# Second weight matrix loaded and used in two halves, all down projections ahead of all up projections, and the last batch's residual finished inside the recurrence

## The reference

```
c = layernorm(cond) * gamma + beta
w = gelu(c @ W1 + bias1) @ W2 + bias2            # W2 is 256 x 8192, 8 MB
a1, b1, a2, b2 = split(w, 4)                     # each [B, D, 8], per batch
mid = gelu(x @ base_down + (x @ a2) @ b2.T)      # "down"
out = mid @ base_up.T + (mid @ b1) @ a1.T        # "up"
x2  = x + (x + out)
for t in range(512):                             # recurrence over time, all 4 batches
    h = tanh(x2[:, t] @ Wx + b + h @ Wh)
    result[:, t] = x2[:, t] + h
```

## Time and profile before

| | |
|---|---|
| median of 3 runs | 568.85 us (566.21 to 568.97) |
| the profiled execution, its own time | 569.51 us |
| its span, first to last instruction | 567.6 us |
| PE busy | 510.9 us (90%) |
| DVE, ACT, POOL busy | 287.8, 173.9, 21.6 us |
| recurrence's first own product (L653) starts | 79.80 us |

### The profile page before, as it was taken

How to read it: one execution, slowest core, us unless ns; L and a number is a source line. 1 busy time by engine, 2 the same in 40 slices (tenths; PEclk the granted TensorE clock), 3 DMA queues, 4 the chain that set the end, 5 groups by cost and what they waited for, 6 DMA issues and landing times.

```text
span 567.6 us, 31977 instructions
## 1 busy us (share of the span) xinstructions
PE 510.9 (90%) x14200; PEld 429.1 (76%) x14200; DVE 287.8 (51%) x2214; ACT 173.9 (31%) x1128; POOL 21.6 (4%) x33
## 2 busy tenths in 40 slices
PE   4979989999999999999999999999999999999995
PEld 4334458888888888888888888888888888888884
DVE  2142355555555555555555555555555555555553
ACT  3021113333333333333333333333333333333322
POOL 1039100000000000000000000000000000000000
PEclk9978989999999999999999999999999999999999
DMA  7950000000000000000000000000000000000000
GB/s 259 387 190 0 0 3 4 4 13 5 13 4 13 4 14 4 13 5 10 8 3 14 3 14 3 14 3 14 3 14 3 13 5 14 3 11 6 6 13 12
DMA packets 11216, 15.99 MB, mean 28 GB/s; under 512 B 1587, under 2 KB 6978, under 8 KB 11074
## 3 DMA queue, kind: packets, MB, share of 16 engines
q1 hardware_dynamic: 11078, 13.95, 7.4%
HBM read 11.85 MB, written 2.10 MB: 25 GB/s over the span
## 4 chain that ended last, share of the span: by engine, by line
PE 82%; ACT 8%; issue 3%; SPq 3%; DMA 3%; DVE 0%; DVEq 0%
PE bank L653 66%; ACT w_sb L358 8%; PE bank L633 7%; PE bank L589 3%; DMA w_sb<-in_L_cond_W 3%; PE bank L601 2%; SPq L227 2%; PE bank L642 1%; PE bank L628 1%; PE bank L571 1%; PE bank L578 1%; PE bank L515 0%; PE bank L554 0%; ACT xT L315 0%; DVE x2T L446 0%
## 5 line engine op out<-in xcount | busy, mean ns | idle before, releaser
L653 PE MATMUL bank<-w_sb,whp 128*128 128x52 bf16 x6132 | 244.2, 186 | 38.7 <-ACT w_sb L358 38.0
L653 PEld LDWEIGHTS bank<-w_sb,whp 128*128 128x128 bf16 x6132 | 188.5, 96 | 86.8 <-ACT w_sb L358 64.5
L479 DVE TENSOR_TENSOR r_ring<-w_sb 128x4 f32<-128x4 f32 x1022 | 136.6, 164 | 220.9 <-ACT w_sb L358 218.5
L358 ACT ACTIVATE w_sb<-bank 128x4 f32<-128x4 f32 x1024 | 142.2, 174 | 324.7 <-PE bank L653 324.7
L653 PE MATMUL bank<-r_ring,whp 128*128 128x52 bf16 x4096 | 220.7, 186 | 0.0
L653 PEld LDWEIGHTS bank<-r_ring,whp 128*128 128x128 bf16 x4096 | 174.7, 96 | 0.0
L653 PE MATMUL bank<-l_ring,whp 128*128 128x52 bf16 (+1 forms) x2048 | 157.5, 178 | 0.0
L484 DVE TENSOR_TENSOR l_ring<-r_ring 128x4 bf16<-128x4 f32 x1024 | 135.9, 162 | 0.0
L653 PEld LDWEIGHTS bank<-l_ring,whp 128*128 128x128 bf16 x2048 | 122.3, 96 | 0.0
L633 PE MATMUL bank<-xp,wxp 128*128 128x32 bf16 x1536 | 76.2, 176 | 0.0
L633 PEld LDWEIGHTS bank<-xp,wxp 128*128 128x128 bf16 x1536 | 56.2, 95 | 0.0
(11 more groups left out here) (84 smaller groups left out, 147.6 us busy)
## 6 DMA issues: line engine op xcount, KB each, us to landing
w_sb<-in_L_cond_W SPq DMA_DIRECT2D x8, 1024.0 KB, 14.0
x_sb<-in_x SPq DMA_DIRECT2D x4, 512.0 KB, 9.6
out<-o_sb SPq DMA_DIRECT2D x64, 32.0 KB, 1.6
w_sb<-in_L_cond_W SPq DMA_DIRECT2D x1, 256.0 KB
up_sb<-in_L_cond_base_up SPq DMA_DIRECT2D x1, 256.0 KB, 3.1
down_sb<-in_L_cond_base_down SPq DMA_DIRECT2D x1, 256.0 KB, 11.1
wh_sb<-in_L_cond_Wh SPq DMA_DIRECT2D x1, 256.0 KB
wx_sb<-in_L_cond_Wx SPq DMA_DIRECT2D x1, 256.0 KB
```

The costliest lines, as they stand in the source:

```text
L358: nc.scalar.activation(h_ring[:, m, slot(pair, s), 0:B], zt, ACT.Tanh).then_inc(h_ready, 1)
L479: nc.vector.tensor_tensor(r_ring[:, k, q, 0:B], state_before(pair, s, k)[:, 0:B], state_hi_before(pair, s, k)[:, 0:B], ALU.subtract).then_ ...
L653: return nc.tensor.matmul(zbank(p, q, m)[:, col0:col0 + n], whp[part][:, k, P * m:P * (m + 1)], rhs[:, 0:n], start=False, stop=stop, skip_ ...
```

## The change

1. **W2 in two halves.** Types A2 and B2 of all chunks are loaded first (eight transfers of 0.5 MB), then x1, base_down, x2, x3, then A1 and B1 of all chunks. The PE's products follow: `w_products(0, c)` takes A2 and B2, `w_products(1, c)` A1 and B1. DVE's keep_rank works on the 64 partitions of one half.
2. **Two queues.** ACT issues cond, gamma, beta, bias2, W1, bias1, b, x0 and base_up at its start. SP starts with W2 at once. `ld_cond` is now cond alone; gamma and beta, and W1 and bias1, have semaphores of their own.
3. **Order on the PE.** The bias2 products go ahead of the first layer's. The x0 and base_up transposes stand between the first half's W products. All low_down, all down, the second half's W products between the downs, all low_up, then the four ups. midT lies over x_sb and has room for four batches; x transposes use two banks in place of three.
4. **The last batch's x2.** DVE makes only its first 64 steps (`FIRST`) ahead of the recurrence, and the other 448 in eight pieces of 112 in the steps 3 to 10 of the first pair.
5. **Smaller moves.** POOL makes quadrant and splits b first; the padding of h_ring comes last. ACT, not DVE, copies upT. DVE makes facm for A2 alone and b1m itself, a batch at a time, in place of one operation over all and ACT's copy.

```diff
+        HALVES = ((A2, B2), (A1, B1))
...
+            def load_w2(h):
+                j = min(HALVES[h])
+                for c in range(NCH):
+                    for k in range(K2):
+                        sp.dma_start(w2_sb[:, k, j:j + 2, CH * c:CH * (c + 1)],
+                                     w2v[k, :, j:j + 2, CH * c:CH * (c + 1)]).then_inc(ld_w2[h][c][k], 16)
+
+            load_w2(0)
+            load_x(1)
+            sp.dma_start(down_sb[:], base_down.rearrange("(k p) n -> p k n", p=P)).then_inc(ld_down, 16)
+            load_x(2)
+            load_x(3)
+            load_w2(1)
...
+            def w_products(h, c):
                 for k in range(K2):
-                    pe.wait_ge(ld_w2[c][k], 16)
-                    for j in range(NTYPE):
+                    pe.wait_ge(ld_w2[h][c][k], 16)
+                    for j in HALVES[h]:
                         last = nc.tensor.matmul(bank[c][Q * j:Q * (j + 1), :],
...
-            dve.wait_ge(ld_cond, 80)
+            dve.wait_ge(ld_cond, 16)
...
+                    if b < B - 1:
+                        make_x2(b, n, 0, T).then_inc(x2_ready, 1)
+                    else:
+                        make_x2(b, n, 0, FIRST).then_inc(x2_first, 1)
...
+                    if first and PIECE0 <= s < PIECE0 + PIECES * K2:
+                        n, i = (s - PIECE0) % K2, (s - PIECE0) // K2
+                        make_x2(B - 1, n, FIRST + (T - FIRST) // PIECES * i,
+                                FIRST + (T - FIRST) // PIECES * (i + 1)).then_inc(x2_rest, 1)
```

More of the change, by code:

```diff
@@ L130, in adaptive_lowrank_then_recurrence @@
         ld_cond = sem("ld_cond")
+        ld_gb = sem("ld_gb")
+        ld_w1 = sem("ld_w1")
         ld_bias2 = sem("ld_bias2")
         ld_x = [sem(f"ld_x{b}") for b in range(B)]
-        ld_base = sem("ld_base")
-        ld_w2 = [[sem(f"ld_w2_{c}_{k}") for k in range(K2)] for c in range(NCH)]
+        ld_down = sem("ld_down")
+        ld_up = sem("ld_up")
+        ld_w2 = [[[sem(f"ld_w2_{h}_{c}_{k}") for k in range(K2)] for c in range(NCH)] for h in range(2)]
+        ld_b = sem("ld_b")
         ld_rnn = sem("ld_rnn")
@@ L152, in adaptive_lowrank_then_recurrence @@
         upT_ready = sem("upT_ready")
-        ld_up = sem("ld_up")
-        w_ready = sem("w_ready")
-        facm_ready = sem("facm_ready")
+        w_ready = [sem(f"w_ready{h}") for h in range(2)]
+        a2_ready = sem("a2_ready")
         b1_ready = sem("b1_ready")
@@ L320, in _ @@
                                      bias=bias1_sb[:, m:m + 1]).then_inc(g_ready, 1)
-            for g in range(B * K2):
+            move_transposes(0)
+            move_transposes(1)
+            act.wait_ge(upT_psum, 1)
+            nc.scalar.copy(upT[:].rearrange("p k n -> p (k n)"), bank[6][:]).then_inc(upT_ready, 1)
+            for g in range(K2, B * K2):
                 move_transposes(g)
-            act.wait_ge(facm_ready, 1)
-            nc.scalar.copy(b1m[:], facm[Q * B1:Q * (B1 + 1)]).then_inc(b1_ready, 1)
             for b in range(B):
@@ L328, in _ @@
                     act.wait_ge(mid_psum, K2 * b + m + 1)
[L329 to L332, removed]
+                    nc.scalar.activation(midT[:, b, m, :], mid_bank(b, m)[:], ACT.Gelu).then_inc(mid_ready, 1)
             def x_part1(col0):
@@ L361, in states @@
                         if s % TS == 0:
+                            if 2 * pair + s // TS + 1 == FIRST // TS:
+                                act.wait_ge(x2_rest, PIECES * K2)
                             if 2 * pair + s // TS > 2:
@@ L424, in _ @@
-            dve.wait_ge(ld_base, 16)
-            def add_down(b):
+            for b in range(B):
+                nc.vector.tensor_scalar(facm[Q * A2:Q * (A2 + 1), b], fac[Q * A2:Q * (A2 + 1)],
+                                        bmask[Q * A2:Q * (A2 + 1), b:b + 1], None, ALU.mult).then_inc(a2_ready, 1)
+            dve.wait_ge(ld_down, 16)
+            for b in range(B):
                 dve.wait_ge(wd_psum, b + 1)
-                nc.vector.tensor_tensor(wd[:, b].rearrange("p k n -> p (k n)"), bank[4 + b][:],
+                nc.vector.tensor_tensor(wd[:, b].rearrange("p k n -> p (k n)"), low_bank(b)[:],
@@ L428, in add_down @@
                                         down_sb[:].rearrange("p k n -> p (k n)"), ALU.add).then_inc(wd_ready, 1)
-            def add_up(b):
+            for c in range(NCH):
+                keep_rank(1, c)
+            for b in range(B):
+                nc.vector.tensor_scalar(b1m[:, b], fac[Q * B1:Q * (B1 + 1)], bmask[Q * B1:Q * (B1 + 1), b:b + 1],
+                                        None, ALU.mult).then_inc(b1_ready, 1)
+            dve.wait_ge(upT_ready, 1)
+            for b in range(B):
@@ L508, in _ @@
             last.then_inc(condT_ready, 1)
-            def transposes(g):
-                if g >= 3:
-                    pe.wait_ge(tr_moved, g - 2)
-                for i in range(NTT):
-                    last = nc.tensor.transpose(tr_bank(g)[:, P * i:P * (i + 1)],
-                                               x_sb[:, g // K2, i, P * (g % K2):P * (g % K2 + 1)], ident[:])
-                last.then_inc(tr_ready, 1)
+            pe.wait_ge(ld_bias2, 16)
+            pe.wait_ge(quadrant_ready, 1)
+            for c in range(NCH):
+                nc.tensor.matmul(bank[c][:], quadrant[:].rearrange("j i q -> j (i q)"),
+                                 bias2_sb[:, CH * c:CH * (c + 1)], start=True, stop=False, skip_group_check=True)
             pe.wait_ge(cn_ready, 1)
@@ L688, in recurrence @@
                                 pe.wait_ge(o_ready, pair)
+                        if first and p == 0 and i == 4:
+                            pe.wait_ge(x2_rest, PIECES * K2)
                         input_products(1 - p, i // 4, i // 2 % 2, [i % 2])
```

210 lines of the change are left out of this document (110 added, 100 removed).

## The result

The changed kernel takes 572.86 us (median of 12 executions, 570.20 to 574.77), the kernel before 568.84 (12 executions, 566.21 to 569.52). The ratio is 1.0073, with a 95% interval of 1.0051 to 1.0096: slower by 4.0 us where 4.3 us less were forecast. The profiled execution of the changed kernel took 574.48 us, its span is 572.6.

The account below looks back on a forecast made before the run. The recurrence's start was taken as bound by W2's landing, the PE work behind it and TensorE's clock. Summed steps put the last x2 at 73.75 instead of 78.02, 4.3 us earlier, so 564.6 us; range 561.0 to 576.5.

Parts of the forecast that it names:

- down 0 to the end of the last up: PE preparation: downs and ups 27.4, second half of W 6.9, low_up 3.5, half clock 3.4 us.
- 5.2 at the latest: Latest landing of bias2's transfer, taken from base_up's 3.1 us; 4.7 was assumed, in a span of 4.4 to 5.2.
- Costs that I take as nothing: List of effects counted as zero: x2 pieces in the recurrence, shared transfers, POOL's padding, and last fac, b1m and wu.
- with 18 us to spare: POOL's h_ring padding waits for the second half, ending near 50, and takes 5.2 us, with that much slack.
- the last fac, b1m and wu lie under down 2 and down 3: Claim that these late preparation operations are covered by PE's downs and cost nothing.
- clock term: 3.4 us added between down 0 and the last up for a half-clock stretch like the one before.
- Rival A: TensorE's clock stays at 1.2 GHz through the first half of W products: last x2 at 83.9, 574.8 us; chance 0.31.
- rival B: Clock rises late, after the first half's third quarter: 3 us more, 567.6 us; chance 0.12.
- rival C: Clock doesn't fall ahead of down 0: 3.4 us gained, 561.2; chance 0.07 together with an early rise from bias2 products.
- go by the row: bias2 products assumed not to raise the clock, as measured before: 564.6 us, against 562.1 if they did.
- The doubled rounds: W products in halves run two passes side by side: sixteen more rounds, 6.9 us at full clock.
- The pieces: Last x2's eight 112-column operations, some 0.36 us each, hidden behind DVE's waits in the recurrence; 2.9 us if not covered.

Follow-up runs that it names:

- e2: Changed kernel with bias2 as SP's first transfer, ahead of W2, instead of fourth on ACT's queue: 569.22 us, 1.0014 of the kernel before.
- e4: Changed kernel with all nine of ACT's transfers issued from SP ahead of W2: 570.91 us, 1.0032 of the kernel before.
- e7: Changed kernel with b1m made by four scaled copies on ACT instead of DVE, padding where it was: 569.56 us, 1.0045 of the kernel before.
- e3: Changed kernel with POOL's h_ring padding waiting for the last wu and bias2 first on SP: 563.34 us, 0.9932 of the kernel before.
- e1: Changed kernel with POOL's h_ring padding waiting for the last wu instead of the last W product: 566.90 us, 0.9984 of the kernel before.
- e5: On e3, two column chunks of a half multiplied together, so four passes run side by side: 558.90 us, 0.9845 of the kernel before.
- e6: On e3, the last batch's x2 made whole ahead of the recurrence, without the eight pieces: 563.70 us, 0.9929 of the kernel before.

## Why the prediction was wrong

The sum was to end with the last x2 at 73.75 and ended at 83.92, 10.2 us later. By its own steps, in the profiled execution:

| step | forecast | measured | off |
|---|---|---|---|
| bias2 products start | 4.7 | 7.92 | +3.2 |
| from there to the first W product | 10.1 | 10.3 | +0.2 |
| first half | 10.8 | 12.0 | +1.2 |
| from there to down 0 | 6.6 | 7.3 | +0.7 |
| down 0 to the end of the last up | 41.2 | 46.1 | +4.9 |
| last x2 | 0.3 | 0.3 | 0 |

**The first step that failed** is "5.2 at the latest" for bias2. The bound was taken from base_up's 3.1 us in the kernel before, a transfer with little ahead of it: while it was under way (3.2 to 6.3) the DMA engines moved 223 GB/s. After the change eight transfers of W2 are issued from 0.73 on, the engines move 315 to 351 GB/s from 2 to 7.9, and bias2, issued at 1.96, takes 5.9. e2 and e4 show that this is their company: sent ahead of W2, from either place in the order, it is there in time. The prediction did say that W1 shares the engines with W2, and gave it room, but not bias2. The Trainium skill, "DMA: Bandwidth & Descriptors", section "Issuing engines are not separate DMA queues", says that transfers of all issuing engines run on the same 16 DMA engines and interleave, and that a second issuer saves issue time only. The traces agree: on a queue of its own beside W2 bias2 took 5.9 us, and ahead of W2 on W2's queue (e4) 2.6.

**The second** stands under "Costs that I take as nothing": POOL's padding, "with 18 us to spare", and "the last fac, b1m and wu lie under down 2 and down 3". Both were judged alone. The padding waits for the second half, and so does b1m; the one starts at 52.09 and the other at 53.50. That they would meet was to be seen from the diff, and nothing of the trace of before shows a price for it, since its POOL memset lay beside DVE operations that read PSUM (`L427`, 0.69 each) and began (37.96) when facm had ended (37.79). The Trainium skill, "SBUF — State Buffer", section "Who interferes with whom", states the rule: DVE and GpSimd share a pair of ports, a `tensor_scalar` can enter the mode that takes it, and whoever comes second "fully blocks"; an operation with one input in SBUF outside that mode and a `tensor_reduce` do not contend, and ACT waits for nobody. The rows agree: b1m (tensor_scalar) 3.95 us in place of 0.33, the reduction L450 inside the same memset 0.68, L427 inside the memset of before 0.69, ACT's b1m in e7 0.49. The rule was there to be weighed and wasn't.

Of the 4.9 us between down 0 and the last up 1.9 are the PE's wait for b1m. 1.7 are clock: 3.4 forecast, 5.1 measured (10.2 us at half the rate). The 1.3 left are small gaps: e3, without wait or fall, has the same 1.3, and in its chain each of the four downs takes 3.63 us where the sum had 3.42 (the ups take 3.44), the second half 7.1 for 6.9, the low_ups 3.65 for 3.5. By e1 the wait and the clock behind it are worth 6.0 us in the medians (5.1 by the ratios), by e2 the landing of bias2 3.6 (3.4), and e3 takes back both, 9.5 (8.0). e3 lands at 563.3, beside the 564.6 of the forecast, but with other terms, so this is in part luck. Its profiled execution took 562.4 us where the sum, ahead of the step to the median, had 565.2: no clock term (3.4 less), bias2 0.7 earlier, 0.7 less in the recurrence, and the 2.0 of gaps more.

**Rival A** (the clock stays at 1.2 GHz) fell in every run that has two side by side: the clock rose behind them, 6.1 us into the W products after the change and 3.2 in e2. The forecast had 4.1, and the two us more at half the rate are 1.0 of the 1.2 us that the first half took longer, a small form of rival B. Rival A's numbers are nearly the measured ones (last x2 at 83.9, 574.8 us; the profiled execution has 83.92 and 574.48), and it is to make room for A that the range reached up to 576.5. That agreement is coincidence, since nothing of A's mechanism happened. The bias2 products did not raise the clock in their new place either: 7.2 us without a gap, and the first W products still 0.85 apart. There the prediction was right to go by the row. That the clock does not fall ahead of down 0 was rival C's claim, and it was right on the place. The fall came later, and cost more than the one that it replaced.

**What held.** The doubled rounds cost what was said: the second half took 7.1 us beside 6.9, and e5 gets 4.4 of it back net. W2 left the chain. The pieces cost nothing: in the trace after the change they take 0.35 us each in the steps 3 to 10, and those steps are 0.94 us apart as the later ones are. From the bias2 products to the first W product, and from the first half to down 0, the sum is right within 0.7.

**What stays open** is what makes the clock fall. In the changed kernel it fell in every execution, and without the wait in one of 12 (e1). In e2, e4 and e7, with the wait, it fell in all. That shows that the wait brings it on in this place. (For executions without a trace, this is read from the mean clock.) But e5 had a fall behind an almost unbroken stretch, and e3 in two of nine executions. In the five traces with a fall (the changed kernel, e2, e4, e5 and e7) it lies among the low_up products or right behind them, 0.9 to 4.4 us after the first; e1, e3 and e6 run the same products without one. So the wait is one way to it, together with the low products that follow, and not the only one. A part of the run to run spread, up to 4 us here, is the length of such stretches, and no run tells what decides it.

## What to carry to other kernels

When a change moves a long GpSimd operation or one on VectorE, lay the two engines' rows side by side: here a tensor_scalar on SBUF that started under a memset of 5 us ended with it. A small transfer on which the first long block of work depends goes ahead of the bulk loads, whichever engine issues it. And an edit that takes a transfer off the path (here W2) is worth what the next thing lets through: read the waits behind it with their new neighbours, not with the old ones.

## What was not expected of the hardware

- A VectorE operation of 0.33 us took 3.95 beside a GpSimd memset, and ended 0.14 us behind it; in e5 four of them took 2.78 in place of 1.13 beside GpSimd's elementwise operations.
- A PE wait of 1.9 us was followed by 10.2 us at 1.2 GHz in one profiled execution and by 6.8 in another (e2); the six shorter executions of the changed kernel are 3.3 us below the six longer.
- A round of two quarter-width fp32 products takes as long as one of four, 0.43 us.
